# Unit-scaled keys and queries against raw ones with per-token factors, and a chunk's three inverse applications summed in PSUM

## What is computed

```python
q, kk, v = silu(conv4(x @ W_qkv.T))                # causal convolution over 4 tokens
q, kk = l2norm(q), l2norm(kk)                      # a / max(sqrt(sum(a * a)), 1e-12), per head and token
beta, decay = sigmoid(b_raw), exp(-exp(A_log) * softplus(a_raw + dt_bias))
def step(state, t):
    state = state * decay_t
    delta = (v_t - k_t @ state) * beta_t
    state = state + outer(k_t, delta)
    return state, q_t @ state
y = o * silu(z)
y = y * rsqrt(mean(y * y) + 1e-6) * norm_w         # per value head and token
out = y @ W_out.T
```

## Time and profile before

| | |
|---|---|
| median of the runs | 1953.5 us |
| the profiled execution, its own time | 1959.84 us |
| its span, first to last instruction | 1957.8 us |
| mean granted TensorE clock | 0.969 |
| busy: PE, DVE, ACT, POOL | 1751.0, 1523.7, 1226.5, 635.2 us |
| ACT_TABLE_LOAD of `rnorm` and `scale_y` | 96 of 1.283 us |

### The profile page before, as it was taken

One profiled execution on the slowest core, in us unless ns is written; L12 is line 12 of the kernel. 1 busy time (PEld: TensorE's weight loads), 2 busy tenths in 40 slices (PEclk: granted clock), 3 DMA queues, 4 the chain that ended last, 5 costly groups with the idle time before them and its releaser, 6 DMA issues.

```text
span 1957.8 us, 33489 instructions
## 1 busy us (share of the span) xinstructions
PE 1751.0 (89%) x12824; PEld 1303.0 (67%) x12824; DVE 1523.7 (78%) x2421; ACT 1226.5 (63%) x2155; POOL 635.2 (32%) x442
## 2 busy tenths in 40 slices
PE   7899999999989879988988999888998899988976
PEld 5676676767656556766766667666776666766765
DVE  7888888888774787888878878788787887877853
ACT  3343535344445567778777777778777786777762
POOL 2213222222230536145153250532614416144140
PEclk9999999999999889999999999999999999999988
DMA  3010111101032001101111011010110101101000
GB/s 132 32 63 31 62 43 49 62 31 62 1 99 67 17 1 40 48 23 34 39 39 33 23 33 50 28 33 23 34 55 23 33 23 33 55 23 33 7 2 22
DMA packets 51445, 75.37 MB, mean 39 GB/s; under 512 B 3393, under 2 KB 41793, under 8 KB 51185
## 3 DMA queue, kind: packets, MB, share of 16 engines
q1 hardware_dynamic: 51312, 73.55, 11.8%
HBM read 72.29 MB, written 1.25 MB: 38 GB/s over the span
## 4 chain that ended last, share of the span: by engine, by line
PE 37%; DVE 14%; ACT 13%; issue 5%; POOL 3%; POOLq 0%; ACTq 0%; DVEq 0%
PE bank L725 6%; PE bank L891 6%; PE bank L846 5%; DVE d_sil L1305 5%; POOL d_dec L1623 3%; PE bank L736 3%; DVE d_Rb L1371 2%; PE bank L784 2%; DVE d_X L1357 2%; DVE d_W L1379 2%; PE bank L794 2%; ACT d_V L1104 2%; PE bank L867 1%; PE bank L798 1%; PE bank L868 1%
## 5 line engine op out<-in xcount | busy, mean ns | idle before, releaser
L1305 DVE SCALAR_TENSOR_TENSOR d_sil<-d_pre,d_w,d_sil 128x1024 f32<-128x1024 f32 x192 | 298.1, 1553 | 5.9 <-ACT d_pre L1075 5.6
L1629 POOL TENSOR_TENSOR d_Rb<-d_V,d_ones 128x512 bf16<-128x512 f32 x32 | 51.6, 1631 | 705.6 <-ACT d_V L1104 705.6
L1357 DVE CAST_PREDICATED d_X<-tables_sb,bank 128x512 bf16<-128x512 int32 x192 | 134.4, 700 | 154.8 <-PE bank L784 152.3
L725 PE MATMUL bank<-xnT,d_w 128*128 128x512 f32 x480 | 246.9, 650 | 0.4
L189 PE MATMUL bank<-xnT,a_w 128*128 128x512 f32 x512 | 237.5, 598 | 0.0
L1139 ACT ACTIVATE d_T<-bank 128x512 bf16<-128x512 f32 x160 | 98.5, 616 | 115.4 <-PE bank L794 113.0
L846 PEld LDWEIGHTS bank<-d_W,d_N 128*128 128x128 f32 x1024 | 122.7, 193 | 35.0 <-DVE d_W L1379 22.4
L1623 POOL TENSOR_TENSOR d_dec<-d_dec,d_qk 128x384 f32<-128x384 f32 x128 | 134.3, 1075 | 35.0 <-DVE d_N L1338 35.0
L725 PEld LDWEIGHTS bank<-xnT,d_w 128*128 128x128 f32 x480 | 90.5, 204 | 79.9 <-issue 79.9
L189 PEld LDWEIGHTS bank<-xnT,a_w 128*128 128x128 f32 x512 | 91.0, 192 | 78.8 <-issue 78.8
L489 POOL TENSOR_TENSOR a_hidc<-a_hid,a_comb 128x512 f32<-128x512 f32 x32 | 44.5, 1392 | 295.0 <-DVE a_hid L336 295.0
(11 more groups left out here) (211 smaller groups left out, 4495.6 us busy)
## 6 DMA issues: line engine op xcount, KB each, us to landing
d_dec<-decay_scratch SPq DMA_DIRECT2D x32, 512.0 KB, 5.9
a_w<-w SPq DMA_DIRECT2D x16, 897.0 KB, 4.5
d_w<-w SPq DMA_DIRECT2D x16, 776.0 KB, 4.8
a_comb<-comb_scratch SPq DMA_DIRECT2D x16, 512.0 KB, 5.5
d_dec<-decay_scratch SPq DMA_DIRECT2D x32, 256.0 KB, 6.2
d_wo<-w SPq DMA_DIRECT2D x16, 256.0 KB, 3.1
f_w<-w SPq DMA_DIRECT2D x8, 256.0 KB, 4.0
tables_sb<-tables SPq DMA_DIRECT2D x1, 1056.0 KB, 9.2
```

The costliest lines, as they stand in the source:

```text
L725: last = pe.matmul(psum[bank][:, :], cols(slot, (c * KT + k) * P, P), xnT[:, k, h * HALF:(h + 1) * HALF], start=(k == 0), stop=(k == KT - 1))
L1305: dve.scalar_tensor_tensor(sil[c][:, :, :], pre[c % 2][:, :, tap:tap + S], cols(slot, OC + 4 * c + tap, 1), sil[c][:, :, :], ALU.mult, ALU ...
L1357: dve.copy_predicated(left(Xp[lv][:, v], lv), mask.unsqueeze(1).broadcast_to([P, 8, 64]).rearrange("p n (g w) -> p n g w", w=lv), psum[4 + ...
```

## The change

Keys and queries are no longer scaled to unit length. With |k| the norm of a token's key, the kernel keeps the raw products and puts the factors elsewhere:

- `norms` now multiplies the squares, 128 tokens at a time, with a ones tile of 64 columns, so that the sums stand with the token on the partition: 16 matmuls of 64 columns instead of 4 of 512. Every 64th column is read.
- `guard` makes from these three 128x8 tiles: the guarded sums of the keys, a term for the queries, and the reciprocals `krec`. ACT takes one Sqrt (`key_norm`) after `copy_qk(3)`.
- `matrices` and `copy_qk` multiply the columns' factor `krec` in, by chunk, so each is two instructions (128x256 and 128x128) instead of one.
- POOL multiplies V by |k| after `decayed(3)`: Rb (128x512) and then V itself (128x1024), for each value head. The former L1629 at the head's start is gone.
- The query's norm goes into the epsilon of the output norm (`mean_y`). That norm is now Sqrt on ACT (`root_y`) and a reciprocal on DVE (`inverse_y`), which stands in level 0 of the inversion.
- `rnorm` and both `unit` go.
- The three `apply` of a chunk accumulate in their bank. W is then a copy of the bank each time: value head 0's by ACT (`next_w`), value head 1's by DVE (`update`, now `tensor_copy`).
- `project_z` of quarters 0 and 1 no longer waits for `guard`.

```diff
             def project_z(slot, i, n):
-                pe.wait_ge(s["max_done"], i * 2 + n // 2 + 1)
+                if n < 2:
+                    pe.wait_ge(s["pre_done"], i * 8 + 5 + n)
+                    need(pe, s["acc_done"], (i - 2) * 4 + 3 + n)
+                elif n == 2:
+                    pe.wait_ge(s["kss_done"], i * 2 + 2)
+                else:
+                    pe.wait_ge(s["kss_done"], i * 2 + 1)
...
             def norms(i, c, h):
-                pe.matmul(psum[2 * c + h][:, :], onesf[:, :], nrm[c][:, h * HALF:(h + 1) * HALF],
-                          start=True, stop=True).then_inc(s["ssq_ready"], 1)
+                for t in range(4 * h, 4 * h + 4):
+                    last = pe.matmul(psum[2 + c][:, t * 64:(t + 1) * 64], sq[c][:, t * P:(t + 1) * P], onesf[:, 0:64],
+                                     start=True, stop=True)
...
                 for b in range(B):
                     last = pe.matmul(psum[4 + 2 * v][:, b * P:(b + 1) * P], TT[v][:, 2 * b + c, :], Rb[v][:, b, :],
-                                     start=True, stop=True)
+                                     start=(a == 0 and b == 0), stop=(a == 2), skip_group_check=True)
...
-                pe.wait_ge(s["kq_done"], i * 2 + 2)
+                pe.wait_ge(s["sil_done"], i * 4 + 2)
                 products(i, 0)
...
+            def key_norm(i):
+
+                act.wait_ge(s["kss_done"], i * 2 + 1)
+                need(act, s["vb_done"], i * 4)
+                act.activation(knorm[:, :], kss[:, :], ACT.Sqrt).then_inc(s["knorm_done"], 1)
...
+            def next_w(i, c, a):
+                act.wait_ge(s["apply_ready"], i * 12 + 6 * c + 2 * a + 1)
+                act.activation(Wv[0][:, :, c, :], psum[4][:, :].rearrange("p (b d) -> p b d", b=B),
+                               ACT.Copy).then_inc(s["wup_done0"], 1)
...
-            def update(i, v, c, a):
-                ww = Wv[v][:, :, c, :]
-                dve.tensor_tensor(ww, ww, psum[4 + 2 * v][:, :].rearrange("p (b d) -> p b d", b=B),
-                                  ALU.add).then_inc(s["wup_done"], 1)
+            def update(i, c, a):
+                dve.wait_ge(s["apply_ready"], i * 12 + 6 * c + 2 * a + 2)
+                dve.tensor_copy(Wv[1][:, :, c, :], psum[6][:, :].rearrange("p (b d) -> p b d", b=B)).then_inc(s["wup_done1"], 1)
...
+            def guard(slot, i):
+                dve.wait_ge(s["ssq_ready"], i * 2 + 2)
+                need(dve, s["knorm_done"], i)
+                dve.tensor_scalar(kss[:, :], psum[3][:, 0:HALF:64], 4e-24, None, ALU.max).then_inc(s["kss_done"], 1)
+                dve.tensor_scalar(qeps[slot][:, :], psum[2][:, 0:HALF:64], 4e-24, 16e-6, ALU.max, ALU.mult).then_inc(s["kss_done"], 1)
+                dve.wait_ge(s["kss_done"], i * 2 + 1)
+                need(dve, s["qk_done"], i * 4)
+                dve.reciprocal(krec[:, :], kss[:, :]).then_inc(s["krec_done"], 1)
...
             def body(j, slot, i):
                 nxt = after(j, slot, i)
-                for v in range(2):
-                    pool.wait_ge(s["v_done"], i * 4 + 2 * v + 2)
-                    pool.tensor_tensor(Rb[v][:, :, :], V[v][:, :, 0, :], onesf[:, :].unsqueeze(1).broadcast_to([P, B, P]),
-                                       ALU.mult).then_inc(s["vb_done"], 1)
...
+                pool.wait_ge(s["knorm_done"], i + 1)
+                scale = knorm[:, :].rearrange("p (b c) -> p b c", c=2).unsqueeze(3).broadcast_to([P, B, 2, P])
+                for v in range(2):
+                    pool.wait_ge(s["v_done"], i * 4 + 2 * v + 2)
+                    pool.tensor_tensor(Rb[v][:, :, :], V[v][:, :, 0, :], scale[:, :, 0, :], ALU.mult).then_inc(s["vb_done"], 1)
+                    pool.wait_ge(s["vb_done"], i * 4 + 2 * v + 1)
+                    pool.tensor_tensor(V[v][:, :, :, :], V[v][:, :, :, :], scale, ALU.mult).then_inc(s["vb_done"], 1)
```

135 lines of the change are left out of this document (64 added, 71 removed).

## The result

The changed kernel took **1927.7 us** (median of 4 runs, 1925.4 to 1928.7) against 1953.9 (4 runs, 1953.2 to 1955.6): ratio 0.9863, 95% interval 0.9846 to 0.988. The forecast was 1927.6 in a range of 1908 to 1949. The sum comes out closer than its terms: one of them (`inverse_y`) missed by 0.59 us in each of 14 heads, and others missed the other way, so most of what follows is about the terms.

A forecast was written before the change was run, and what follows sets the result against it. No engine is full; a head is a relay of waits between engines. Inner heads -1.67 us each, times 14 -23.4, head 0 +1.5, head 15 and the tail -4.0: -25.9 from 1953.5 gives 1927.6, range 1908 to 1949.

The forecast's parts named there:

- `inverse_y`: Level 0 of the inversion, where DVE sets the pace: one added narrow instruction, +0.20 us per inner head.
- Products: Products of an inner head: split copies cost +0.25 and +0.3, one load and two Sqrt save 1.25; sum -0.70 us.
- The table load at the Tanh: End of the inversion: the load carries the wait for the output projection, so it is serial on ACT; +1.28 us per head.
- Rival 2: A table switch holds ACT longer than its row: 1.28 us more in 15 heads, +19, 1947 us; chance 0.06.
- Applications: First half: one DVE copy replaces two additions in two steps, -1.20 us; second half: z's projection starts without its wait, -0.95.
- rival 1: ACT's copies of W come late in the applications, so half of the 2.15 goes: +15, 1943 us; chance 0.15.
- POOL, 0 predicted: POOL's longer queue ends 32.0 us after DVE's first predicated copy; the mask is needed at 35.0, 3.0 to spare: 0.
- Rival 4: POOL's mask ends after ACT's decays need it, 4.6 us late, each microsecond costing 14: 1992 us; chance 0.09.
- Clock: Wait before the first corner shortens by 0.7 us; a fifth of the 1.4 us a head lost to falls returns: -0.3.
- Rival 3: The shorter wait no longer lets PE's clock fall in any head: the full 1.4, 15 us more, 1912; chance 0.12.
- Head 0: First head: no output norm to save, both loads, its end hanging on POOL's MLP tail; +1.5 us.
- Head 15 and the tail: Last head and the norm behind it: products -1.0, +0.2, four application steps -2.0, norm -1.2; together -4.0 us.

## Why the prediction was right, step by step

**Products, -0.70 predicted, -0.77 measured.** ACT's split copy takes 0.75 from its start to the load's, where one took 0.51: +0.24 for +0.25. One load and two Sqrt take 1.55 (1298.67 to 1300.22) for 2.95 in the same view (1309.14 to 1312.09): -1.40, where I had -1.25, from 3.04 by the chain. DVE's split of `d_kk` is 0.48 and 0.34 us long, and `d_N` behind it starts 0.77 after its start where it was 0.58, so +0.19 each for +0.15. These add up to -0.78, the measured stage.

**The table load at the Tanh, +1.28 predicted, +1.23 measured** by taking it away. The argument that it carries its function's wait, from the order of instructions, is shown by the row at 1330.78. Rival 2, and the 2.66 that the Trainium skill (ScalarE: Activation LUTs, What ACT_TABLE_LOAD costs) gives for a switch, do not hold here: the row is 1.28 and the time it held up is 1.23.

**`inverse_y`, +0.20 predicted, +0.79 measured by moving it: the step that was furthest off.** I costed the instruction and not what it releases. The instruction itself is 0.25, and the narrow `d_gcol` behind it fell from 1.04 to 0.11, so by themselves the two are no cost at all. But POOL's `scale_y` waits for it and so moved from ahead of the inversion to beside two convolutions on which the levels' chain runs, +0.60 and +0.63 on them. "More POOL beside DVE slows the convolution" stood in the prediction, but was looked for at the end of the inversion and costed at nothing there. Of the levels' +1.82 the two terms give 1.23 + 0.79 = 2.02; with both away the levels are 28.12, 0.19 under before.

The Trainium skill (SBUF — State Buffer, Terms) has DVE and GpSimd exclude one another on their port pair, the loser fully blocked. The trace agrees, and the prediction misread it. It set the 1.12 us that a convolution lost against POOL instructions of 1.98, the mean of four, and found less than a full block. One by one they are not alike. At the same place of the next head, beside the mask in the earlier trace rows, the convolution takes 2.40 again, and the POOL instruction that it met is 1.28 long:

```profile
1327.68 1.28 POOL L1609 TENSOR_TENSOR d_dec<-d_dec,tables_sb 128x512 f32<-128x512 f32 x1
```

It ends at 1328.96, and the convolution, from 1327.64, at 1330.04: 1.08 after it, as in the rows of the changed kernel above. What a convolution loses is what was left of the POOL instruction that it met, and a POOL instruction loses what was left of the convolution (2.76 for 1.90 in the scaling of V).

**Applications, -1.20 and -0.95 predicted, -2.21 together measured.** The first is 1.19 by the kernel with both copies on DVE. The second, by the wait put back, belongs to the narrow guards. Where the prediction wrote that `rnorm` and `unit` "count no further", it left out a condition (rival 1 had half of it, "`rnorm` leaves there"): without their removal the last copy's wait holds up `rnorm`, and the sum in PSUM makes the kernel slower by 0.6%. The value of that removal cannot be read from the waits of before, because there `rnorm` was on time.

**POOL, 0 predicted.** It ended 33.6 us after the first copy, not 32.0. With the clock up it was needed at 35.3 (35.0 predicted): 1.64 to spare for 3.0; in heads with a fall it was needed at 36.0. The end came out as near as it did because errors cancelled: `scale_y` 4.73 for 3.75, the two `decayed` 5.84 for 3.88 and the scaling of V 2.62 on average for 1.88, against 12.9 for 15.85 in the identity and the mask. Rival 4 did not come about. Its point of decision is right to within that, and its price of 14 us a microsecond is too high: lateness of 1.25 us cost nothing through ACT, and with two instructions more the decays waited 43.0 us in all for 20.6 of time.

**Clock, -0.3 predicted, -0.66 measured.** The direction was right, and its reason only in part. I expected fewer falls; there were more, and each cost less. Rival 3 was wrong for this kernel, and its mechanism right: with PE's waits filled the time is 1918.3, where I had 1912.

**Head 0, +1.5 predicted, +0.7 measured. Head 15 and the tail, -4.0 predicted, -6.1 measured.** Products -0.77 for -1.0, levels -0.96 for +0.2 (no Tanh follows, so no load; PEclk was 0.81 and 0.83 there, and what made the rest of it was not tried), applications -1.28 for -2.0, and the rest -3.1 for -1.2. In that rest the output projection's 32 matmuls took 9.24 us in before and 7.16 after, pieces of the chain of waits of each:

```profile
1929.73 8.32 issue
...
1942.69 9.24 PE bank L891 x32
```

```profile
1901.83 7.35 issue
...
1913.82 7.16 PE bank L903 x32
```

The wait ahead of them is 1 us shorter, as predicted for the load, and the clock came back up sooner: PEclk is 0.83 for 0.67 in the two tail windows at the top, and PE is busy for 10.92 us for 13.00 with the same 48 matmuls. That is another 2 us which no term held. Why it rose sooner was not tried.

The sum: 14 × 1.82 = 25.5, less 0.7, plus 6.1 is 30.9, and the profiled executions are 31.0 apart. The prediction added its terms from rows of that same slow execution and got 25.9, which is 5.0 too little for it: 2.1 in the heads, 0.8 in head 0, 2.1 in the tail. Subtracted from the median instead, it met a difference of 26.2. That the two agree to 0.3 is luck: an underestimate of 5 met a profiled execution of before that lay 6 above its median. The mechanism was right in its large terms, and the range of 1908 to 1949 did not need the luck: 1953.5 less the measured 30.9 is 1922.6.

## What to carry to other kernels

Cost an instruction that is moved by what it releases as well as by its own length: here 0.25 us on DVE let POOL's work start beside the chain's longest DVE instructions, and each of the two engines then stood for what was left of the other's instruction. Read such rows one by one; a mean over four hides it. A table load waits with the function behind it, so where a function stands behind a wait, one column of the same function ahead of that wait moves the load into idle time (17 us here for one line). Giving an engine with a strict queue more work pays only if what stands last in that queue is early enough: a copy of 0.6 us that waits 4.2 holds all behind it for 4.2. Look up who waits for the last item before moving anything ahead of it. And measure a small step with the clock kept up: the early `inverse_y` was worth nothing without that and 17 us with it.

## What the runs showed of the chip beyond expectation

TensorE's level decided more than any single term. With PE idle for 1.04 us ahead of the first corner and 0.93 behind it, in an otherwise busy stretch, it still fell in 13 of 14 heads. Seven matmuls that compute nothing kept it at 2.4 GHz in all heads, worth 9.4 us in the changed kernel and 19 to 21 in the one before. A fall cost 0.8 us in the changed kernel and 2.3 with `inverse_y` earlier, so that a stage made 0.8 us shorter gained nothing. How often it falls does not follow from the length of a stage in any way that I could work out: one more POOL instruction, which left products and levels as long as they were, took it from 13 heads to 4.

A narrow DVE instruction can lose far more than its own length to POOL. `d_gcol` of 16 columns is 1.04 us in before, where POOL runs `decayed`, and 0.11 in the changed kernel, where POOL stands idle for `inverse_y` at that moment; with `inverse_y` ahead of the levels and POOL at work again it is 0.84. DVE's row and POOL's of that kernel:

```profile
1383.51 0.84 DVE L1400 TENSOR_SCALAR d_gcol<-col_g 128x16 f32<-128x16 f32 x1
```

```profile
1383.32 1.00 POOL L1637 TENSOR_TENSOR d_dec<-d_dec,d_qk 128x384 f32<-128x384 f32 x1
```

It ends at 1384.35, 0.03 after the POOL instruction that it met. That fits the exclusive port pair of the Trainium skill (SBUF — State Buffer, Terms), as the convolutions do. Which DVE instructions are held in this way, and which are not, no run here set out to measure; the predicated copies that write X and read a bank take 0.68 to 0.75 in the changed kernel, beside POOL or not.
